# One stage in TensorE's loop, edges of a chunk in two parts, and 64 instead of 112 nodes for each sum by dst

## The reference

```
dx = max(edge_attr_2[:, 0], 1e-6);  inv_dx = 1/dx;  slope = edge_attr_2[:, 1] * inv_dx
diff = (x[dst] - x[src]) * inv_dx
d1 = segment_sum(diff, dst) - segment_sum(diff, src)
S  = segment_sum(slope, dst)
u  = x - clip(dt) * (x * d1 + g * S)
x  = layernorm(x + u)
x  = layernorm(x + segment_sum(edge_attr_16, dst) / max(count by dst, 1))
```

## Time and profile before

| what | value |
|---|---|
| runs | 5037.35, 5045.37, 5047.1 us |
| profiled execution | 5042.16 us, of which the span is 5040.3 us |
| TensorE matmul busy | 4590.3 us, 91% |
| VectorE busy | 3983.5 us, 79% |
| GpSimd busy | 3415.4 us, 68% |
| ScalarE busy | 1446.6 us, 29% |
| mean granted TensorE clock | 0.975 |
| first and last stage of TensorE begin at | 112.8 us and 4960.4 us |

### The profile page before, as it was taken

The page is one execution under the profiler, slowest core; times in us unless marked ns, Lnnn a source line. Parts: engine busy times, 40 slices in busy tenths (PEclk is TensorE's granted clock), DMA queues, the critical chain, the costliest instruction groups (busy, mean ns, idle before and its releaser), DMA issues. The chain is left out here.

```text
span 5040.3 us, 72091 instructions
## 1 busy us (share of the span) xinstructions
PE 4590.3 (91%) x31379; PEld 1240.2 (25%) x12630; DVE 3983.5 (79%) x8600; ACT 1446.6 (29%) x1018; POOL 3415.4 (68%) x3133
## 2 busy tenths in 40 slices
PE   1999999999999999999999899999999999999997
PEld 0222222222222222222222222222222222222222
DVE  4887778778877787778887787778787788787887
ACT  3322232222322232222322233222322233222320
POOL 5667667767677677676677667767676776776760
PEclk8999999999999999999999999999999999999998
DMA  3111111111111111111111111111111111111110
GB/s 75 31 36 35 31 31 31 40 31 31 31 32 39 31 31 31 39 31 31 31 31 39 31 31 31 32 39 31 31 31 38 33 31 31 31 39 31 31 29 7
DMA packets 210295, 167.87 MB, mean 33 GB/s; under 512 B 124650, under 2 KB 193774, under 8 KB 210024
## 3 DMA queue, kind: packets, MB, share of 16 engines
q1 hardware_dynamic: 109798, 139.79, 8.7%
q0 software_dynamic: 100000, 25.80, 6.6%
q10 hardware_dynamic: 476, 2.01, 0.1%
HBM read 164.55 MB, written 2.81 MB: 33 GB/s over the span
## 5 line engine op out<-in xcount | busy, mean ns | idle before, releaser
L412 POOL DMA_INDIRECT x_src<-in_x_dram,src_i x3125 | 3410.5, 1091 | 1492.9 <-issue 871.0
L635 PE MATMUL ps_src<-hi_hot,spread_lo 128*128 128x392 bf16 x18750 | 4210.7, 332 | 77.7 <-issue 75.9
L947 DVE TENSOR_SCALAR hi_hot<-col_h,hi_f,scale 128x1568 bf16<-128x1568 f16 x3125 | 2238.7, 723 | 482.0 <-remote 270.3
L630 PE MATMUL ps_src<-hi_hot,spread_lo 128*128 128x392 bf16 x6250 | 2075.6, 332 | 210.0 <-issue 140.4
L630 PEld LDWEIGHTS ps_src<-hi_hot,spread_lo 128*128 128x128 f16 x6250 | 620.7, 99 | 1319.2 <-issue 952.8
L882 DVE TENSOR_TENSOR spread_lo<-spread_lo,halves 128x640 f16<-128x640 f16 x1250 | 616.8, 494 | 60.1 <-issue 59.9
L583 PEld LDWEIGHTS ps_w<-dst_of_node,parts 128*102 128x102 bf16 x3125 | 392.3, 126 | 1050.9 <-issue 1011.6
L572 PEld LDWEIGHTS ps_x<-xwin,node_of_dst 112*128 112x128 bf16 x3125 | 305.8, 99 | 1358.3 <-issue 1348.7
L572 PE MATMUL ps_x<-xwin,node_of_dst 112*128 112x48 bf16 x3125 | 584.5, 190 | 49.2 <-issue 41.7
L583 PE MATMUL ps_w<-dst_of_node,parts 128*102 128x112 bf16 x3125 | 501.3, 213 | 51.4 <-DVE parts L871 41.5
L482 ACT CAST parts<-pay 128x425 bf16<-128x425 f32 x125 | 72.4, 579 | 1616.0 <-DVE pay L846 1500.7
(11 more groups left out here) (114 smaller groups left out, 1200.5 us busy)
## 6 DMA issues: line engine op xcount, KB each, us to landing
rel_all<-rel_d SPq DMA_DIRECT2D x125, 800.0 KB
x_src<-in_x_dram,src_i POOLq DMA_INDIRECT x3125
a<-in_edge_attr_dram SPq DMA_DIRECT2D x125, 200.0 KB
a<-in_edge_attr_dram SPq DMA_DIRECT2D x125, 25.0 KB
src_i<-in_src_dram SPq DMA_DIRECT2D x125, 12.5 KB
dst_i<-in_dst_dram SPq DMA_DIRECT2D x125, 12.5 KB
xwin<-xparts_d SPq DMA_DIRECT2D x125, 10.5 KB
dst_sum<-in_dst_dram SPq DMA_DIRECT2D x1, 1400.0 KB
```

The lines of the kernel that those rows point to most:

```text
L412: nc.gpsimd.indirect_dma_start(x_src[:, b, j * F:(j + 1) * F], None, x[:, :], bass.IndirectOffsetOnAxis(ap=src_i[:, b, j:j + 1], axis=0)). ...
L630: return nc.tensor.matmul(out_bank, weights, moving, start=False, stop=stop)
L635: return nc.tensor.add_instruction(mybir.InstMatmult(name=nc.get_next_instruction_name(), engine=pe.engine, start_tensor_calc=False, stop_ ...
L947: v.tensor_scalar(hi_hot[:, slot(b, j), :], col_h[:, :], hi_f[:, b, j:j + 1], scale[:, b, j:j + 1], ALU.is_equal, ALU.mult).then_inc(hi_ho ...
```

## The change

- TensorE's loop body is one stage, run C-2 = 123 times. `node_of_dst`, `dst_of_node`, `xwin` and `spread` exist once, and the slot of `hi_hot` is `j % 13`, of which 12 are used ahead (RING, LEAD = 13, 12).
- A chunk's edges lie in two parts: tiles 0 to 12 hold the first 1664 edges, tiles 13 to 24 the other 1536. Each part's sums by dst have a window of SWIN = 64 nodes with a base of its own and go to columns 0 to 63 and 64 to 127 of the PSUM bank. VectorE adds them with two instructions. Each load of src, dst and the edge attributes becomes two DMAs.
- `spread` is handed over in five groups of five tiles (`spread_ready`). Six of its ten instructions stay in the stage before, four come in the stage that uses them (after one-hots 2, 3 and 8).
- New tables `base_tab2`, `sums_tab`, `shift_all`; TensorE and VectorE each read a second count a chunk (`sums_span`).
- SyncE loads `xwin` and `rel_all` ahead of the edge attributes, and ScalarE's `node_hot` waits for the rows of the chunk before.

```
-    RING = 10
+    SPLIT = J // 2 + 1
+    SWIN = 64
+    GROUPS = ((0, SPLIT), (SPLIT, J))
+    RING, LEAD = 13, 12
...
-    PIECES = {0: ["x_of_dst"], 1: ["x_in", "attr_parts", "dst_rel", "dst_hot"], 2: ["dst_hot"], 3: ["dst_hot"], 4: ["dst_hot"], 5: ["dst_hot", "diff"],
-              6: ["pay", "lo"], 7: ["scale"], 8: ["scaled"], 9: ["left"], 10: ["parts"],
-              12: ["spread"], 13: ["spread"], 14: ["spread"], 15: ["spread"], 16: ["spread"], 17: ["spread"], 18: ["spread"],
-              19: ["spread"], 20: ["spread"], 21: ["spread"], 22: ["slope"], 24: ["window", "attr_left"]}
+    EARLY = 3
+    LATE_AT = {2: 1, 3: 1, 8: 2}
+    PIECES = {0: ["x_of_dst"], 1: ["x_in", "attr_parts", "rel2", "dst_hot"], 2: ["dst_hot"], 3: ["dst_hot"], 4: ["dst_hot"], 5: ["dst_hot", "diff"],
+              6: ["pay", "lo"], 7: ["scale"], 9: ["scaled"], 10: ["left"], 11: ["parts"], 12: ["dst_rel"],
+              14: ["spread"], 15: ["spread"], 17: ["spread"], 18: ["spread"], 21: ["spread"], 22: ["spread", "slope"], 24: ["window", "attr_left"]}
...
 def reload_edges(m, b):
-    sp.wait_ge(dst_hot_ready, m + 1)
+    sp.wait_ge(dst_rel_ready, m + 1)
     load_dst(m + 2, b)
+    sp.wait_ge(x_dst_ready, m + 1)
+    load_window(m + 1)
+    sp.wait_ge(node_diff_ready, m + 2)
+    load_rel(m + 2)
     sp.wait_ge(slope_ready, m + 1)
     load_a2(m + 2, b)
-    sp.wait_ge(node_diff_ready, m + 2)
     sp.wait_ge(attr_left_ready, m + 1)
     load_a16(m + 2, b)
-    load_rel(m + 2)
-    sp.wait_ge(x_dst_ready, m + 1)
-    load_window(m + 2, b)
...
 def node_hot(m, b):
-    act.wait_ge(x_dst_ready, m - 1)
+    act.wait_ge(x_dst_ready, m)
...
 def finish(n):
     act.wait_ge(scaled_ready, n + 1)
+    act.wait_ge(spread_ready, n * FIVES)
...
 def take_sum(hots, j):
-    return nc.tensor.matmul(ps_w[0:SPL * V, 0:WIN], parts[:, j, :, :].rearrange("p k v -> p (k v)"),
-                            hots[:, j, :], start=(j == 0), stop=(j == J - 1))
+    q, (lo, hi) = [(q, g) for q, g in enumerate(GROUPS) if g[0] <= j < g[1]][0]
+    return nc.tensor.matmul(ps_w[0:SPL * V, q * SWIN:(q + 1) * SWIN], parts[:, j, :, :].rearrange("p k v -> p (k v)"),
+                            hots[:, j, 0:SWIN], start=(j == lo), stop=(j == hi - 1))
...
-def stage(c, b, k_next, finish, begin):
+def stage(c, finish, begin):
     if finish:
-        span = further_rows(c + 1)
-    pe.wait_ge(chunk_ready, c + 1)
+        further_rows(c + 1)
+        span = sums_span(pe, c + 1)
     for j in range(J):
+        if j % 5 == 0:
+            pe.wait_ge(spread_ready, c * FIVES + (j // 5 + 1))
...
-with pe.Fori(0, PAIRS) as i:
-    for b in range(2):
-        stage(i * 2 + b, b, i + 1, True, True)
-stage(C - 3, 0, PAIRS + 1, True, True)
-stage(C - 2, 1, 0, True, False)
+with pe.Fori(0, C - 2) as i:
+    stage(i, True, True)
+stage(C - 2, True, False)
...
 if piece == "window":
+    span = sums_span(dve, n)
     dve.wait_ge(win_sum_ready, n + 1)
-    win = dst_sum[0:SPL * V, ds(base, WIN)]
-    v.tensor_tensor(win, win, ps_w[0:SPL * V, 0:WIN], ALU.add).then_inc(win_added, 1)
+    win = dst_sum[0:SPL * V, ds(base, SWIN)]
+    step(v.tensor_tensor(win, win, ps_w[0:SPL * V, 0:SWIN], ALU.add))
+    settle_here()
+    win = dst_sum[0:SPL * V, ds(base2, SWIN)]
+    v.tensor_tensor(win, win, ps_w[0:SPL * V, SWIN:2 * SWIN], ALU.add).then_inc(win_added, 1)
...
+def spread_half(n, five, q):
+    if q == 0:
+        dve.wait_ge(hi_hot_free, n * J + (five * 5 + 5 + LEAD - J))
+    tiles = slice(five * 5, five * 5 + 5)
+    ins = v.tensor_tensor(spread[:, tiles, q, :, :], lo_rows[:, tiles, :, :], bc(halves[:, tiles, q, :], 2, LO), ALU.mult)
+    if q == HLV - 1:
+        ins.then_inc(spread_ready, 1)
```

More of the change, by code:

```diff
@@ L235, in later, with this, sums_span @@
                                       skip_runtime_bounds_check_because="windows are counted up to the one that holds the greatest dst")
+        def this(base, g, first):
+            return nc.s_assert_within(base + (g - first) * WIN, 0, NODES - 1,
+                                      skip_runtime_bounds_check_because="windows are counted up to the one that holds the greatest dst")
+        def sums_span(eng, c):
+            return nc.values_load_multi_w_load_instructions(sums_tab[0:1, ds(c, 2)], engines=[eng.engine], min_val=0, max_val=C * (NODES // WIN + 1))[1]
         def further_span(eng, c):
@@ L483, in finish @@
                 act.wait_ge(scaled_ready, n + 1)
+                if not (isinstance(n, int) and n == 0):
+                    act.wait_ge(spread_ready, n * FIVES)
                 nc.scalar.copy(halves[:, :, 0, :], scaled[:, :, :]).then_inc(half0_ready, 1)
@@ L589, in sums, with wide_sums, x_of_dst @@
                 return last
-            def x_of_dst(m, k, b):
-                pe.wait_ge(win_loaded[b], k * 16 + 16)
+            def wide_sums(hots):
+                for j in range(J):
+                    last = nc.tensor.matmul(ps_w[0:SPL * V, 0:WIN], parts[:, j, :, :].rearrange("p k v -> p (k v)"),
+                                            hots[:, j, :], start=(j == 0), stop=(j == J - 1))
+                return last
+            def x_of_dst(m):
+                pe.wait_ge(win_loaded, m * 16 + 16)
                 pe.wait_ge(node_hot_ready, m + 1)
-                take_rows(node_of_dst[:, b, :, :], xwin[0:WIN, b, :]).then_inc(x_dst_ready, 1)
+                take_rows(node_of_dst, xwin[0:WIN, :]).then_inc(x_dst_ready, 1)
             def further_rows(n):
@@ L609, in further_rows, with window_sums @@
                 return span
-            def window_sums(n, b, span, first=False):
+            def window_sums(n, span, first=False):
                 pe.wait_ge(dst_hot_ready, n + 1)
@@ L616, in window_sums @@
                     pe.wait_ge(win_added, n)
-                sums(dst_of_node[:, b, :, :]).then_inc(win_sum_ready, 1)
+                sums(dst_of_node).then_inc(win_sum_ready, 1)
                 further_sums(span)
@@ L645, in tile @@
                 for k in range(HLV):
-                    weights = spread[:, b, j, k, :, :].rearrange("p l f -> p (l f)")
+                    weights = spread[:, j, k, :, :].rearrange("p l f -> p (l f)")
                     for q in range(4):
-                        last = (matmul_again if q else first_matmul)(ps_src[:, q, 0:HB], weights, hi_hot[:, slot(b, j), q * HB:(q + 1) * HB],
+                        last = (matmul_again if q else first_matmul)(ps_src[:, q, 0:HB], weights, hi_hot[:, slot(j), q * HB:(q + 1) * HB],
                                                                      stop and k == HLV - 1)
@@ L653, in tile @@
                     for s in range((j - SUM_AT) * 3 + first, (j - SUM_AT) * 3 + first + count):
-                        if sums_of is not None and 0 <= s < J:
-                            one = take_sum(dst_of_node[:, sums_of, :, :], s)
+                        if does_sums and 0 <= s < J:
+                            one = take_sum(dst_of_node, s)
                             if s == J - 1:
@@ L658, in tile @@
                     r = (j - ROWS_AT) * 2 + k
-                    if rows_of is not None and 0 <= r < J:
-                        one = take_row(node_of_dst[:, rows_of, :, :], xwin[0:WIN, rows_of, :], r)
+                    if does_rows and 0 <= r < J:
+                        one = take_row(node_of_dst, xwin[0:WIN, :], r)
                         if r == J - 1:
@@ L946, in one_hot, with late @@
                     dve.wait_ge(hi_hot_free, c * J + j + min(HOTS_FREE, J - j))
-                v.tensor_scalar(hi_hot[:, slot(b, j), :], col_h[:, :], hi_f[:, b, j:j + 1], scale[:, b, j:j + 1],
+                v.tensor_scalar(hi_hot[:, slot(j), :], col_h[:, :], hi_f[:, b, j:j + 1], scale[:, b, j:j + 1],
                                 ALU.is_equal, ALU.mult).then_inc(hi_hot_ready, 1)
+            def late(c, j):
+                for _ in range(LATE_AT.get(j, 0)):
+                    at = done.setdefault("late", 0)
+                    done["late"] += 1
+                    spread_half(c, EARLY + at // 2, at % 2)
             def stage(c, b, k_next, k_later, tiles, does_finish, does_begin, pieces=PIECES):
@@ L961, in stage @@
                         one_hot(c, b, j)
+                        late(c, j)
                     for piece in pieces.get(j, []):
```

278 lines of the change are left out of this document (161 added, 117 removed).

## The result

The changed kernel takes 5106.2 us (median of 4 runs, 5101.98 to 5118.27) beside 5046.24 us of the kernel before: a ratio of 1.0124, with a 95% interval of 1.0099 to 1.0148. It is slower by 60 us. The forecast was 50 us faster, and the range ended at 5090.

What follows compares the result with a forecast made beforehand. TensorE, busy 91%, was taken as the bound, VectorE not far behind. From the profiled 5042 us, -50 + 20 + 8 + 5 - 35 + 3 = -49 gave 4993, with 3 us to the median 4996 us; range 4640 to 5090.

Steps and rivals of the forecast that it cites:

- D: TensorE's loop with one stage a body: 62 more branches back cost 5 us (0 to 19); no code fetched.
- A: TensorE's sums by dst with 64 columns instead of 112: saves 50 us, bounds 0 and 66.
- E: SyncE's order: loading rel_all and xwin earlier may move or spread stalls; saves 35 us, bounds 0 and 160.
- B: VectorE's order: four late spread instructions delay one-hots, mostly hidden by the ring; costs 20 us, bounds 0 and 123.
- C: The second count read on TensorE's queue each stage: costs 8 us, 148 bare, 0 hidden.
- F: Single buffers (node_hot, dst_of_node) cost 0; some twenty tiny VectorE instructions in the setup cost 3 us.
- rival 1: TensorE's stalls go with its long loop body or two bodies' registers: 4647 us; chance 0.18.
- Rival 3: Nothing seen: A's gain is eaten by B and C, E gives nothing; within 10 us of 5045; chance 0.11.
- Rival 2: VectorE's late spreads make TensorE wait at tiles 8 to 13: 5131 us, middle about 5080; chance 0.29.

Runs made afterwards that it cites:

- e5: The changed kernel as it stands, timed where the kernel before takes 4500.27 us: 4624.25 us, ratio 1.0278.
- e1: The changed kernel without VectorE's two loops for further windows, which this data never enters: 4501.14 us, ratio 1.0002 to the kernel before.
- e12: The changed kernel as it stands, timed where the kernel before takes 5051.66 us: 5130.47 us, ratio 1.0143.
- e13: The changed kernel with 64 one-column memsets at VectorE's start, timed where the kernel before takes 5051.66 us: 5078.15 us, ratio 1.0041.
- e3: The kernel before with 19 never-run memsets added in each of VectorE's stages (body 264 to 302 instructions): 4627.82 us, ratio 1.0287.
- e4: The kernel before with sums by dst over 64 of 112 columns, other nodes left out: 4455.85 us, ratio 0.9902.
- e7: The changed kernel with 32 one-column memsets at VectorE's start and gathers released three tiles earlier: 4802.25 us, ratio 1.0672 to the kernel before.
- e16: The changed kernel with 64 one-column memsets at VectorE's start, repeated where the kernel before takes 5034.01 us: 5039.69 us, ratio 1.0008.

## Why the prediction was wrong, point by point

**The step that failed is D**, in the sentence "Code does not come from memory in either body: one instruction packet in 4699 us". The row was right, of the kernel before. I asked it of TensorE, whose body gets shorter, and did not count the body of VectorE, which the change lengthens from 264 to 302 instructions. The term was 5 us, and it measured 123 us in a quick group (e5 against e1) and 52 us in a stalled one (e12 against e13). e3 makes the same loss on the kernel before without executing one more instruction. Without these 52 us the kernel would have taken some 5054 us, inside the range but still no faster: for the sign, A's 50 us and E's 35 us had to fail as well.

The Trainium skill ("Runtime: NRT & Kernel Launch", section "Instruction fetch mechanics") stood in the prediction beside this very step and was put to the wrong engine. Its rule is that a taken branch to a place outside the window held forces a fetch; the rows on VectorE agree (2.53 us ahead of the first one-hot behind the branch back). The section gives most engines a smaller store than TensorE's; no run here shows TensorE's.

**A was right.** 45 us instead of 50, with 35.6 ns a sum (e4). The bound of 29 ns in proportion to the columns was too low; the line through the two rows gave 35. The load of 102 columns of weights fits into these 35 ns, a lower ceiling than the 50 that the earlier trace rows gave.

**B was not far off in size for the spreads and missed the next limit.** It had 20 us; in e5 tile 8 starts 14 us late in all. In e1 no wait of TensorE stands at tiles 9 to 13. The loss of 0.33 us a stage is at tile 8, behind one-hots 6 to 9, and goes with VectorE's 86 us of waits for gathers. GpSimd was at (3323 + 942) / 125 = 34.1 us a chunk in e4 beside a stage of 34.71, so by this estimate a TensorE that gets faster than that gains nothing. I had left GpSimd out, though the page had it at 68% and its issue time makes it nearly full, and had taken the longer ring for pure cover, though the gathers' release hangs on it. That the gathers ate most of A's gain is argued from these rows. The tests of it (earlier gathers) met stalled groups or, in e7, a stage already longer than the gathers need, and it is open.

**C and F, 8 and 3 us in the sum, cost nothing that can be seen.** TensorE's step from tile 24 to tile 0 has no gap in e1. Stage 0 begins at 114.3 us instead of 112.8.

**E gave nothing that can be seen.** No run has the new order of the loads alone. In e13 and e16, with all of A in them, the time is 0.1% to 0.4% over the kernel before. TensorE's own "issue" fell by some 130 us, but its waits for VectorE rose by more. VectorE's "remote" stalls moved from the one-hots (270.3 us, 97 times) to "window" (330.6 us, 52 times), which is a place with less room and not with more; whether the order of the loads did that or the rest of the change is not shown. The stalls aren't the program's own: the changed kernel has them in the profile after the change and none in e5. So neither E's 35 us nor rival 1's 348 us was likely to come from an edit, and the "issue" rows were no sure room to gain from. Where they come from stays open.

**Rival 3 is what is left when the fetches are taken away**: 1.0002 in e1 and 1.0008 to 1.0041 in the stalled groups (the upper end beyond its 10 us). A's gain is eaten, in e1 by what delays tile 8, for the most part the gathers as argued above, and not by C.

**Rival 2 had the sign and the engine, not the mechanism.** TensorE does wait for a late VectorE. But it waits at tiles 0 and 2, where VectorE's queue can't be ahead because "window" holds it until TensorE's last sum, and what makes it late is fetched code, in stalled groups stalls as well, and not the late spreads. Its time of 5131 us also took off A's 50 us, though its own words say that A's gain stands idle then; without them it is 5181 us.

## What to carry to other kernels

Before a loop body grows, count its instructions on each engine, code that is skipped included, and look at the packets of the instruction queue between two moments inside the loop: they were close to zero here as long as it fitted, and 38 instructions more cost 2.8%. When a stall appears right behind a branch back, move the body by some instructions before anything is rewritten; the same body cost 7% or 3% in a quick group by its place alone, and moved further it fetched nothing. And look for a wait that holds an engine in step with another once a stage: idle time ahead of it says nothing of the time behind it.

## What the runs showed of the hardware

- VectorE's loop of 264 instructions runs without fetches, one of 302 with five packets of 8192 bytes a round, or with none, by where it begins: 0 and 32 instructions further it fetches (2.8% and 6.7% over the kernel before), 64 and 96 further it doesn't. Blocks of 128 instructions, four held with the next one fetched ahead, explain all kernels run (302 instructions touch three or four such blocks by where they begin, and five packets a round would be four blocks and the one ahead); this is inferred from the runs, and other explanations weren't excluded. In the trace of e5 the packets inside a stage follow each other after 116 and 109 recorded instructions, to which the skipped ones come. The Trainium skill, in the section named above, has blocks of 256; the packets of half that size and the gaps of 109 and 116 speak for 128 here.
- A branch back that finds its target gone costs VectorE 2.6 us (e5: a median of 2.86 us from the branch to the next instruction of its queue over 61 rounds, against 0.28 us in e1 and 0.30 us in the kernel before).
- The same program, the kernel before, took 4501 us on chip 5 in the first group and 5052 us on the same chip in the fourth. TensorE's granted clock was 0.975 in the stalled profile before, 0.955 in the one after, and 0.993 to 0.996 in the profiles of e1 to e5.
